# Storing q like k: attention scores and maxima as matmuls of 32-row strips

## The reference

```
q, k, v = split(xn @ w_qkv), 16 heads of 8 features
scores  = q k^T / sqrt(8), causal: a later key counts as -1e10
out     = softmax(scores) v;  y = layernorm(out @ w_proj + b_proj + xn) * gamma + beta
experts: softmax of xn @ Wr^T, the best 2 of 8, each gelu(xn W1 + b1) W2 + b2, weighted
```

## Time and profile before

| | |
|---|---|
| time, median of 3 runs | 988.45 us (982.56 to 990.77) |
| profiled execution: span from first to last instruction | 885.8 us |
| median less span | 102.65 us |
| busy: PE / DVE / ACT / POOL | 719.6 / 665.9 / 558.9 / 534.7 us |
| TensorE clock granted, mean | 0.936 of full speed |
| pipelined attention | about 107 to 583 us of the span |
| experts and last pass | about 583 to 886 us |

### The profile page before, as it was taken

How to read it: one execution, slowest core, us unless ns; L and a number is a source line. 1 busy time by engine, 2 the same in 40 slices (tenths; PEclk the granted TensorE clock), 3 DMA queues, 4 the chain that set the end, 5 groups by cost and what they waited for, 6 DMA issues and landing times. The chain is left out here.

```text
span 885.8 us, 26079 instructions
## 1 busy us (share of the span) xinstructions
PE 719.6 (81%) x7698; PEld 521.3 (59%) x7700; DVE 665.9 (75%) x1569; ACT 558.9 (63%) x1125; POOL 534.7 (60%) x724
## 2 busy tenths in 40 slices
PE   0564399999999999999999996659899999999900
PEld 0332256666666666666666664338777878887800
DVE  5858868888988888898888887557566666666635
ACT  0561066767667676766667666548888888888800
POOL 5410167778777777878777777616555556555610
PEclk9985799999999999999999999859999999999965
DMA  8903122232323233232323222402222232222179
GB/s 263 381 2 120 44 83 92 92 105 79 104 78 110 73 110 101 82 102 78 107 78 108 94 88 78 132 19 78 77 70 80 75 81 75 78 74 72 54 243 338
DMA packets 107092, 92.85 MB, mean 105 GB/s; under 512 B 16554, under 2 KB 89394, under 8 KB 107060
## 3 DMA queue, kind: packets, MB, share of 16 engines
q1 hardware_dynamic: 89300, 69.82, 25.5%
q0 software_dynamic: 8704, 17.97, 6.2%
q10 hardware_dynamic: 9056, 4.66, 1.8%
HBM read 43.63 MB, written 48.51 MB: 104 GB/s over the span
## 5 line engine op out<-in xcount | busy, mean ns | idle before, releaser
L578 POOL DMA_INDIRECT parts_dram<-o_T,dest x144 | 144.4, 1003 | 122.2 <-ACT o_T L712 92.4
L630 ACT ACTIVATE probs<-wide 128x1024 f32<-128x1024 f32 x192 | 188.9, 1017 | 33.5 <-PE wide L1055 16.5
L527 POOL DMA_INDIRECT x_slots<-send,send_i x128 | 128.1, 1001 | 71.7 <-POOL send_i L522 40.9
L536 POOL TENSOR_SCALAR_AFFINE_SELECT probs<-probs 128x512 f32<-128x512 f32 (+1 forms) x192 | 146.2, 785 | 27.1 <-ACT probs L630 26.5
L871 DVE TENSOR_REDUCE shift<-bank_maxA 128x2 f32<-128x512 f32 (+1 forms) x192 | 131.9, 687 | 12.3 <-PE bank_maxA L1069 8.5
L687 ACT ACTIVATE probs<-wide,b_all 128x256 f32<-128x256 f32 x288 | 121.1, 477 | 31.2 <-PE wide L1199 30.3
L871 DVE TENSOR_REDUCE shift<-bank_maxB 128x2 f32<-128x512 f32 (+1 forms) x192 | 131.5, 685 | 4.9 <-PE bank_maxB L1069 0.8
L1199 PE MATMUL wide<-lgT,xnT_all 128*128 128x256 f16 x864 | 108.9, 277 | 10.8 <-DVE lgT L970 7.5
L1086 PE MATMUL bank_head<-probs,v_aug 128*32 128x256 f32 (+1 forms) x2048 | 98.3, 333 | 22.6 <-POOL probs L536 22.6
L957 DVE TENSOR_TENSOR probs<-probs 128x512 f16<-128x512 f32 x144 | 99.4, 690 | 4.4 <-ACT probs L693 1.3
L1065 PE MATMUL bank_maxA<-k_cat,q_diag 128*128 128x128 f16 (+1 forms) x512 | 75.9, 251 | 29.1 <-DVE shift L871 17.5
(11 more groups left out here) (171 smaller groups left out, 1305.5 us busy)
## 6 DMA issues: line engine op xcount, KB each, us to landing
qk_rows<-split SPq DMA_DIRECT2D x32, 512.0 KB, 3.2
x_slots<-fill SPq DMA_DIRECT2D x16, 585.0 KB, 7.6
fill<-x_slots SPq DMA_DIRECT2D x72, 130.0 KB
q_diag<-qk_rows SPq DMA_DIRECT2D x256, 32.0 KB
k_cat<-qk_rows SPq DMA_DIRECT2D x64, 128.0 KB
xn_all<-parts_dram SPq DMA_DIRECT2D x8, 1024.0 KB, 11.9
out<-x_all ACTq DMA_DIRECT2D x8, 512.0 KB, 9.6
parts_dram<-o_T,dest POOLq DMA_INDIRECT x144
```

The costliest lines, as they stand in the source:

```text
L527: pool.indirect_dma_start(out=x_slots, out_offset=bass.IndirectOffsetOnAxis(ap=send_i[:, u, c:c + 1], axis=0), in_=send[:, u, c, :], in_of ...
L536: pool.affine_select(out=part, in_=part, compare_op=ALU.is_ge, fill=0.0, base=0, pattern=[[0, n], [1, P]], channel_multiplier=-1).then_inc ...
L578: pool.indirect_dma_start(out=parts_dram, out_offset=bass.IndirectOffsetOnAxis(ap=dest[:, (quad + 2) % 4, t:t + 1].bitcast(U32), axis=0), ...
L630: act.activation(probs[:, u, :], ps[:, :], ACT.Exp, scale=SCALE).then_inc(empty, 1)
```

## The change

q is stored like k, in `q_cat`: one copy, 128 rows, four heads under each other. A head's scores are now a matmul over its 32 rows alone (`strip(j)`), of q as well as of k. The units are cut anew (`SCORES`, `MAXIMA_OF`): a score unit holds two heads j, one in each of its two banks, in two groups (first key tile) or four (second key tile); a maxima unit holds one j. In each maxima unit the mask's matmul is issued first. The score units of the second key tile, which `o0` needs, become s2 and s3. The list has s0 ahead of v and m4, s2 ahead of m7, s3 ahead of m8 and s4 ahead of m10. The second half of q and k is waited for before m4. The clearing of `q_diag` in the prologue goes.

```diff
-        q_diag = sb("q_diag", [P, 2, G, J, T], F16)
+        q_cat = sb("q_cat", [P, 2, G, T], F16)
...
-            ("misc", "v", MAXIMA), ("maxA", "m4", MAXIMA), ("wide0", "s0", SOFT),
+            ("wide0", "s0", SOFT), ("misc", "v", MAXIMA), ("maxA", "m4", MAXIMA),
...
-        SCORES = [(0, (0,)), (0, (1,)), (1, (0, 1)), (0, (2,)), (0, (3,)), (1, (2, 3))]
+        SCORES = [(0, (0, 1), (0, 1)), (0, (2, 3), (0, 1)), (1, (0, 1), (0, 1, 2, 3)),
+                  (1, (2, 3), (0, 1, 2, 3)), (0, (0, 1), (2, 3)), (0, (2, 3), (2, 3))]
+        MAXIMA_OF = [(1, j, (0, 1)) for j in range(J)] + [(1, j, (2, 3)) for j in range(J)] + [(0, j, (0, 1, 2, 3)) for j in range(J)]
+        def strip(j):
+            return slice(ROWS * j, ROWS * (j + 1))
...
-                for j in range(J):
-                    rows = slice(ROWS * j, ROWS * (j + 1))
-                    sp.dma_start(q_diag[rows, par, gs, j, :], qr[j, :, gs, :]).then_inc(half_loaded[h], 16)
-                sp.dma_start(k_cat[:, par, gs, :], kr[:, gs, :]).then_inc(half_loaded[h], 16)
+                for c, cat in enumerate((q_cat, k_cat)):
+                    rows = qk_rows[par, c, :, :, :].rearrange("(g jd) t q -> (jd t) g q", g=G)
+                    sp.dma_start(cat[:, par, gs, :], rows[:, gs, :]).then_inc(half_loaded[h], 16)
...
-                    pool.memset(q_diag[:, :, :, :, :], 0.0).then_inc(consts, 1)
...
+                    for n_, g in enumerate(gs):
+                        for bank_, j in enumerate(js):
+                            at = 512 * bank_ + width * n_
+                            last = M(ps[:, at:at + width], k_cat[strip(j), par, g, P * kt:P * (kt + 1)],
+                                     q_cat[strip(j), par, g, P * kt:T], start=(n_ == 0), stop=(n_ == len(gs) - 1),
+                                     skip_group_check=True)
...
                     M(dst, ident16[:, :], mask16[:, :].rearrange("p (o k) -> p o k", o=1).to_broadcast([P, nh, P]),
-                      start=False, stop=True, skip_group_check=True).then_inc(fill_, 1)
+                      start=True, stop=False, skip_group_check=True)
+                    for n_, g in enumerate(gs):
+                        last = M(ps[:, keys * n_:keys * (n_ + 1)], q_cat[strip(j), 1 - par, g, P * qt:P * (qt + 1)],
+                                 k_cat[strip(j), 1 - par, g, 0:keys], start=False, stop=(n_ == nh - 1), skip_group_check=True)
...
-                        values(0, par, b * 6 + 3)
+                        values(0, par, b * 6 + 4)
...
-                        if what in ("m0", "m6"):
-                            pe.wait_ge(half_loaded[what == "m6"], (s - MAXIMA) * 80 + 80)
+                        if what in ("m0", "m4"):
+                            pe.wait_ge(half_loaded[what == "m4"], (s - MAXIMA) * 32 + 32)
```

More of the change, by code:

```diff
@@ L433, in step @@
                         row = ROWS * j + SHIFT_ROW
-                        sp.dma_start(q_diag[row:row + 1, 1 - par, :, j, :], shift_T[G * j:G * (j + 1), :]).then_inc(shift_loaded, 16)
+                        sp.dma_start(q_cat[row:row + 1, 1 - par, :, :], shift_T[G * j:G * (j + 1), :]).then_inc(shift_loaded, 16)
             steps(sp, step)
@@ L1046, in scores @@
                     ps, fill_ = room(pe, s, f"s{u}")
[L1047 to L1056, removed]
+                    kt, js, gs = SCORES[u]
+                    width = T - P * kt
+                    for n_, g in enumerate(gs):
[4 more added lines that the diff above has]
+                                     skip_group_check=True)
                     last.then_inc(fill_, 1)
@@ L1061, in maxima @@
                     ps, fill_ = room(pe, s, f"m{m}")
[L1062 to L1065, removed]
-                          k_cat[:, 1 - par, g, 0:keys], start=(n_ == 0), stop=False, skip_group_check=True)
-                    nh = len(js)
+                    qt, j, gs = MAXIMA_OF[m]
+                    keys = P * (qt + 1)
+                    nh = len(gs)
                     dst = ps[:, :].rearrange("p (j k) -> p j k", j=nh)[:, :, keys - P:keys]
                     M(dst, ident16[:, :], mask16[:, :].rearrange("p (o k) -> p o k", o=1).to_broadcast([P, nh, P]),
-                      start=False, stop=True, skip_group_check=True).then_inc(fill_, 1)
+                      start=True, stop=False, skip_group_check=True)
+                    for n_, g in enumerate(gs):
+                        last = M(ps[:, keys * n_:keys * (n_ + 1)], q_cat[strip(j), 1 - par, g, P * qt:P * (qt + 1)],
+                                 k_cat[strip(j), 1 - par, g, 0:keys], start=False, stop=(n_ == nh - 1), skip_group_check=True)
+                    last.then_inc(fill_, 1)
                 def values(half_, of, count):
                     ps, fill_ = room(pe, s, f"o{half_}")
-                    first_ = 3 * half_
                     pe.wait_ge(probs_ready, count)
@@ L1080, in values @@
                             for j in range(J):
-                                if kt == 0:
-                                    p_, dst = probs[:, first_ + n_, T * j:T * (j + 1)], ps[32 * j:32 * (j + 1), T * n_:T * (n_ + 1)]
-                                else:
-                                    at = 512 * n_ + P * j
-                                    p_, dst = probs[:, first_ + 2, at:at + P], ps[32 * j:32 * (j + 1), T * n_ + P:T * (n_ + 1)]
+                                unit = next(u for u, (kt_, js, gs) in enumerate(SCORES) if kt_ == kt and j in js and g in gs)
+                                width = T - P * kt
+                                at = 512 * (j % 2) + width * SCORES[unit][2].index(g)
+                                p_, dst = probs[:, unit, at:at + width], ps[strip(j), T * n_ + P * kt:T * (n_ + 1)]
                                 last = M(dst, v_aug[:, of, kt, J * g + j, :], p_, start=(kt == 0), stop=(kt == 1),
```

21 lines of the change are left out of this document (8 added, 13 removed).

## The result

| | before | after |
|---|---|---|
| time, median of 4 runs | 989.61 us (982.56 to 991.88) | 1123.35 us (1121.83 to 1126.66) |
| ratio, 95% interval | | 1.137 (1.131 to 1.143) |
| profiled execution: time, span | (span 885.8) | 1124.25, 1122.5 us |
| TensorE clock granted, mean | 0.936 | 0.819 |

The change costs 134 us; 1093 was predicted, with 1050 to 1130 as the range. The profiled execution of before (span 885.8 us) is some 100 us shorter than every timed run of that kernel, so its steps are no measure of theirs.

A forecast was written before the change was run, and what follows sets the result against it. PE and POOL together, through probs_ready, were taken to bound the 14.16 us step. At 17.7 us a step, 31 steps add 110 us and the prologue saves 5: 988.45 + 110 - 5 = 1093 us, range 1050 to 1130.

The forecast's parts named there:

- The wait at o0: Before values unit o0, PE stands 2.2 us in every step for POOL's fourth mask, which comes behind both sends.
- the sum: Station times from o0 through s0, s2, the sends and mask s3 to the next o0: 17.17 us a step.
- The idle time that was expected ahead of mask s0: A sign to look for in POOL's rows: POOL idle before mask s0; no size given.
- Crossings: On PE, each step between full-height matmuls and 32-row strips costs 0.10 us; 28 new ones, 2.8 us a step.
- Overlap and weight loads: Score strips on PE overlap, 0.21 us a unit instead of 0.43; weight loads of same-row maxima strips charged nothing.
- the rival built on it: Weights of the same strip not loaded ahead: seven inner loads at 0.10 us, 18.4 us a step, about 1115 us; chance 0.05.
- Loads: m4 waits for the second half of q and k: 0.3 us in every other step, taken as 0.2.
- The prologue: Ahead of the first o0, removing the q_diag clearing shortens a stretched DVE operation: -5 us (between 0 and -6.9).
- The clock: Behind o0's wait, PE's clock falls in every fourth step at 1.3 us a fall: 0.3 us a step.
- The rival of a fall in every step: PE's clock falls behind o0's wait in every step: 18.7 us a step, 1124 us; chance 0.10.
- The base: The profiled span of 885.8 us lies 102.65 us below the median of 988.45, a difference carried over unchanged.
- the new loop: The chain o0 to s0 to mask s3 to o0 sets the step: 17.17 us, against 14.16 now.

The follow-up runs named there:

- e4: The kernel before with only its maxima units as 32-row strips, mask first, second half of the loads wanted at m4: 1140.62 us, ratio 1.151.
- e9: The changed kernel with ten matmuls that nobody reads ahead of o0's wait for the fourth mask: 1085.95 us, ratio 1.102.
- e2: The changed kernel with the second sends moved behind mask s3: 1062.27 us, ratio 1.069.
- e5: The kernel before with only the changed kernel's order of PE (list USES): 967.68 us, ratio 0.980.
- b0_again: The kernel before, unchanged, profiled once more: 989.47 us.
- e7: The kernel before with score units alone as strips, o0 behind four masks, sends behind mask s3, and the change's order: 1016.88 us, ratio 1.028.
- e6: The changed kernel with second sends behind mask s3 and neighbouring maxima units issued in pairs: 1061.58 us, ratio 1.076.
- e3: The kernel before with score units alone as strips, o0 behind four masks, sends behind mask s3, old order: 1009.04 us, ratio 1.022.
- e1: The kernel before with one edit, o0 waiting for four masks instead of three, all full height: 1108.75 us, ratio 1.124.
- e11: The kernel before with maxima alone as strips, plus six unread matmuls ahead of m4's wait for the load: 1062.87 us, ratio 1.086.

## Why the prediction was right or wrong

**The wait at o0: right.** 2.11 us, released by POOL's mask in nearly every step, o1 without one. The step from 485.64, in which the clock held, follows the sum station by station (predicted in brackets): m0 at 2.77 (2.82), o1 4.89 (4.82), m2 6.33 (6.26), s0 7.09 (7.20), mask s0 8.93 (8.77), s2 10.21 (10.04), mask s2 11.88 (11.61), mask s3 16.30 (16.04), o0 17.45 (17.17). Timeline of POOL, masks s0, s1, s2, the copy that opens the sends, s3 and s4:

```profile
494.57 0.64 POOL L539 TENSOR_SCALAR_AFFINE_SELECT probs<-probs 128x512 f32<-128x512 f32 x1
...
496.54 0.63 POOL L539 TENSOR_SCALAR_AFFINE_SELECT probs<-probs 128x512 f32<-128x512 f32 x1
...
497.52 1.09 POOL L539 TENSOR_SCALAR_AFFINE_SELECT probs<-probs 128x1024 f32<-128x1024 f32 x1 [0.35 <-ACT probs L633]
...
498.56 0.19 POOL L523 COPY send<-record 128x4 int32 x1
...
501.94 1.74 POOL L539 TENSOR_SCALAR_AFFINE_SELECT probs<-probs 128x1024 f32<-128x1024 f32 x2
```

POOL is idle 0.35 us ahead of mask s2, so PE decides there, as predicted. The idle time that was expected ahead of mask s0 is missing in this step; the steps at a low clock have it (3.26 us at 314.76). Compare: sends between the third mask and the fourth in both.

**Crossings: right.** Timeline of PE after, for the earlier trace rows:

```profile
313.99 0.27 PE L1064 MATMUL bank_maxA<-mask,ident 128*128 128x256 f16 x1
314.20 0.39 PE L1067 MATMUL bank_maxA<-k_cat,q_cat 32*128 32x256 f16 x2
314.52 0.28 PE L1064 MATMUL bank_maxB<-mask,ident 128*128 128x256 f16 x1
```

From the mask to the strips 0.21 us for 0.107 of columns, from the strips to the next mask 0.32 for 0.213: 0.10 and 0.11 at a crossing. PE's own work in the step of 17.45 is 17.45 - 2.06 = 15.4; predicted 15.2. The weight loads show what a crossing looks like: among full-height matmuls a load lies 0.10 us ahead of its matmul, at a crossing it is recorded together with it (488.61 and 488.62, the mask's 256 columns being through at 488.52). So nothing is loaded ahead over a crossing, and PE stands for 0.10 us in it.

**Overlap and weight loads: right.** Eight score strips of 128 columns and a unit of the second query tile with four of its own, timeline of PE after:

```profile
497.35 0.40 PE L1052 MATMUL wide<-q_cat,k_cat 32*128 32x128 f16 x8
497.68 0.39 PE L1064 MATMUL bank_maxA<-mask,ident 128*128 128x512 f16 x1
498.00 0.39 PE L1067 MATMUL bank_maxA<-k_cat,q_cat 32*128 32x128 f16 x4
498.33 0.39 PE L1064 MATMUL bank_maxB<-mask,ident 128*128 128x512 f16 x1
```

1,024 columns in 0.33 us, crossing included, so two strips run at once (one after the other they need 0.43 and the crossing). The four strips of the maxima unit read the same rows, with four weight loads, and take 0.33 for 512 columns: 0.213 and one crossing, nothing between them. The rule of the Trainium skill that was weighed there (TensorE: Matmul & The Clock Gate, Part 3: loads overlap only where the row group differs) does not hold in this trace, and the rival built on it falls.

**Loads: right in direction, less than feared.** SP issues two loads a half (timeline, for the earlier trace rows), and in the steps I looked at m4 waits for none:

```profile
307.46 0.36 SPq L400 DMA_DIRECT2D q_cat<-qk_rows  x1
307.86 0.47 SPq L400 DMA_DIRECT2D k_cat<-qk_rows  x1
```

The 0.2 charged for it was superfluous; with five DMAs (e4) the same wait is 1.04 to 1.57.

**The prologue: direction right, size off.** The DVE operation of 5.77 us in the earlier trace rows now takes 0.17, but the first o0 starts 3.3 us earlier (114.95 against 118.25), not 5.

**The clock: wrong, and this is the step that failed.** I let it fall in every fourth step at 1.3 us, 0.3 a step. After the change it is down in nearly every step: of the 32 o0, two last 1.51 us. Against the step that kept its clock that is 2.9 us a step (20.30 less 17.45). The price was as wrong as the frequency, in every other step: a step of 18.6 costs 1.1 us more than 17.45, which is the 1.3 of the sum, but a step of 22.3 costs 4.9, because its clock stays down for the 12 us of the windows above and not for the 3.6 us that I had put into the estimate from the one fall of the earlier trace rows. From e9, whose mean holds more than that one step, the split of the 4.5 us a step is 2.0 for loop and strips at full clock (17.81 less 15.80) and 2.5 for the clock, against 3.24 and 0.3 of the sum. The rival of a fall in every step had the mechanism and half of its price; that its 1124 us meets 1123.35 is chance, as the next point shows. I had argued that 1.51 us of waiting did nothing and that o0's burst follows each wait. e2 shows a fall behind 1.54. In the change the clock can fall before o0 has begun (the windows around 300.66), so that o0's burst comes too late to hold it. What I overlooked is that the rest of PE's work around the wait had changed too, from full height to strips.

**The base: wrong, and it hid part of that error.** I carried 102.65 us over as if it lay around the span. It lies inside it: half in the attention (15.80 us a step instead of 14.16), half in the experts (351.6 us instead of 301.9), where ACT pauses likewise (48.0 us with no releaser named ahead of its copies L702 and L712, in the profiled before none). The old step being 1.6 us longer, the new loop added only 1.65 at full clock (17.45 less 15.80), not 3.24. Two errors of opposite sign, -1.6 for the loop and +2.6 for the clock, leave +1.0 a step; over 31 steps that, with the 1.7 of the prologue, makes about the 30 us between 1093 and 1123. Split by e9 the two errors are -1.2 and +2.2, with the same sum. That 1093 is only 30 us off is therefore in part luck: most of the two errors cancel.

**Open.** Why the same wait brings the clock down in one kernel and not in another. Shown is a pattern, taken from the pipelined steps: in kernels that are all full height, waits of up to 1.36 us (e5) and 1.78 us (b0_again) left it at 1.00 in every step. Where maxima (e4), scores (e7) or both (e2, e6) are strips, waits of 1.04 to 1.78 us brought it down, in a third of the steps (e7) to nearly all (e4). Score strips with waits of 1.15 us (e3) left it at 1.00. 3.2 to 3.4 us (e1) lowered it at full height as well, and filled pauses kept it up. Whether it is the idle time or the thinner work of the strips around it that decides, no run separates. That strips alone, without any wait, keep it up for good is not shown: e9 still fell at its ends. Open is also ACT's pause without a releaser.

## What to carry to other kernels

Before splitting or reordering units, look at which counted semaphore their consumer waits on and what another engine has queued between the counts: here one number, three masks against four, with two sends between them, cost 12% by itself. Price a new wait on PE twice, as time and as clock, and take the second from rows with the same kind of work around the wait. Where a pause can't be removed, idle banks can take matmuls nobody reads: that gave back 2.5 us a step here (e9, e11), and still left both kernels slower than before. And compare the profiled span with the timed median before using its steps: where they differ by 10%, profile again.

## What the runs showed of the hardware

- A step between full-height matmuls and 32-row strips costs 0.10 to 0.11 us each way. It ate what overlapping saved: 28 crossings by the prediction's count (29 in the trace of the step from 485.64), 2.8 us, against 6 x 0.21 = 1.3.
- Two row strips into two banks overlap fully, and loads for the same strip hide behind its matmuls.
- Once fallen, the clock stayed at 0.50 through uninterrupted work for very different times: some 7 us in e4, 12 us behind the o0 of 300.66 in the change, but only from 323.3 to 326.7 around the next one (323.00). It fell inside a wait (the change) as well as over 1 us after its end (e4).
- The same program had executions 10% apart (the profiled one of before and all the timed ones). In the one long execution profiled, ACT pauses at copies out of PSUM with no releaser that the profile names (2.40 us at 313.62 in b0_again); the short one has no such pauses.
